# Second attention of a four-layer chain: score units in runs of four and eight, key loads released by scores

## The reference, cut to what matters

```python
q = _rmsnorm((x @ Wq).reshape(B, T, H, D), q_rms_w)     # B 4, T 1024, H 16, D 64
k = _rmsnorm((x @ Wk).reshape(B, T, H, D), k_rms_w)
v = (x @ Wv).reshape(B, T, H, D)
gate = softplus(einsum('bthd,hd->bht', k_raw, u_n) / sqrt(D))
bias = where(idx_i >= idx_j, -(idx_i - idx_j) * omega_h * gate_j, -inf)
scores = einsum('bihd,bjhd->bhij', q, k) / sqrt(D) + bias
y = einsum('bhij,bjhd->bihd', softmax(scores), v).reshape(B, T, H * D)
return y @ Wproj
```

## Time and profile before

| quantity | us |
|---|---|
| median of 3 runs | 2235.26 (2231.14 to 2236.41) |
| profiled execution, its own time | 2221.2 |
| its span, first to last instruction | 2219.4 |
| one group of the second attention, steady | 25.27 |
| TensorE busy over the span | 2040.5 |
| VectorE, ScalarE, GpSimd busy | 1351.3, 1148.5, 841.2 |

### The profile page before, as it was taken

The page is one execution under the profiler, slowest core; times in us unless marked ns, Lnnn a source line. Parts: engine busy times, 40 slices in busy tenths (PEclk is TensorE's granted clock), DMA queues, the critical chain, the costliest instruction groups (busy, mean ns, idle before and its releaser), DMA issues.

```text
span 2219.4 us, 34339 instructions
## 1 busy us (share of the span) xinstructions
PE 2040.5 (92%) x11728; PEld 1162.8 (52%) x11728; DVE 1351.3 (61%) x3316; ACT 1148.5 (52%) x1859; POOL 841.2 (38%) x544
## 2 busy tenths in 40 slices
PE   5799999998587998896999999999999999999998
PEld 2333333333486554553566665656656555656644
DVE  4788888884732777874666676666666664333311
ACT  2366666667343686782455555555555553223222
POOL 5000000001501455442677777777777772000000
PEclk8799999999688999996999999999999999999999
DMA  5233333112275689896666777667776687533300
GB/s 180 100 125 121 127 131 130 60 51 74 97 197 142 207 263 332 265 294 162 153 155 163 177 177 177 156 161 180 173 175 163 157 226 210 116 86 86 91 5 10
DMA packets 260300, 335.88 MB, mean 151 GB/s; under 512 B 22732, under 2 KB 181756, under 8 KB 259720
## 3 DMA queue, kind: packets, MB, share of 16 engines
q1 hardware_dynamic: 244824, 305.82, 51.5%
q0 software_dynamic: 7664, 24.39, 3.0%
q10 hardware_dynamic: 7640, 3.48, 0.6%
HBM read 193.69 MB, written 122.62 MB: 143 GB/s over the span
## 4 chain that ended last, share of the span: by engine, by line
PE 41%; issue 6%; DVE 4%; SPq 2%; DMA 1%; ACT 0%; DVEq 0%
PE ps L1287 10%; PE ps L956 6%; PE ps L940 6%; PE ps L909 6%; PE ps L941 5%; PE ps L1238 2%; DVE a1mx L1012 2%; PE ps L1298 1%; PE ps L1275 1%; PE ps L1276 1%; PE ps L943 1%; DVE a1mx L1008 1%; SPq L1162 1%; DMA a1FQ<-s_q 1%; DVE a1mx L1005 0%
## 5 line engine op out<-in xcount | busy, mean ns | idle before, releaser
L1123 POOL TENSOR_TENSOR a1sum<-a1sum,a1prob 128x1024 f32<-128x1024 f32 (+3 forms) x256 | 462.9, 1808 | 82.6 <-ACT a1prob L1066 50.3
L1066 ACT ACTIVATE a1prob<-ps 128x512 f32<-128x512 f32 (+2 forms) x640 | 327.9, 553 | 243.8 <-PE ps L943 209.8
L479 DVE TENSOR_REDUCE a0grid<-ps 128x8 f32<-128x1024 f32 x288 | 351.1, 1223 | 102.1 <-PE ps L351 64.7
L1005 DVE CUSTOM_DVE_ANT_0 ps<-ps,c_mask_ij 128x128 f32<-128x128 f32 x496 | 264.3, 551 | 195.1 <-issue 190.8
L580 ACT ACTIVATE a0prob<-ps 128x1024 f32<-128x1024 f32 x288 | 286.0, 1024 | 168.4 <-PE ps L377 110.9
L940 PE MATMUL ps<-a1QA,a1KA 69*128 69x512 f32 (+3 forms) x768 | 284.6, 378 | 4.4 <-DMA a1QA<-a1neg 4.4
L956 PE MATMUL ps<-a1prob,a1V 128*64 128x512 f32 (+3 forms) x1536 | 273.1, 498 | 4.5 <-ACT a1prob L1066 4.5
L941 PE MATMUL ps<-a1QB,a1KB 128*128 128x512 f32 (+3 forms) x768 | 263.3, 350 | 0.0
L909 PE MATMUL ps<-a1KA,a1QA 68*128 68x128 f32 x744 | 224.7, 381 | 4.8 <-DMA a1KA<-s_g 3.9
L956 PEld LDWEIGHTS ps<-a1prob,a1V 128*64 128x64 f32 x1536 | 102.8, 138 | 172.1 <-issue 138.2
L1008 DVE TENSOR_REDUCE a1mx<-ps 128x1 f32<-128x320 f32 x248 | 145.9, 588 | 70.5 <-PE ps L909 67.6
(11 more groups left out here) (269 smaller groups left out, 3105.1 us busy)
## 6 DMA issues: line engine op xcount, KB each, us to landing
a1FQ<-s_q SPq DMA_DIRECT2D x128, 256.0 KB, 7.9
a1KB<-s_k SPq DMA_DIRECT2D x128, 256.0 KB, 8.6
s_xs<-c_zero POOLq DMA_DIRECT2D x19, 1024.0 KB, 9.4
s_q<-mqkT SPq DMA_DIRECT2D x32, 512.0 KB, 3.6
s_v<-mv SPq DMA_DIRECT2D x32, 512.0 KB, 5.8
s_k<-a1KH SPq DMA_DIRECT2D x32, 512.0 KB, 5.0
s_k<-a1KL SPq DMA_DIRECT2D x32, 512.0 KB, 5.9
a1KA<-s_k SPq DMA_DIRECT2D x64, 256.0 KB
```

Source lines behind the costliest of these rows:

```text
L479: dve.tensor_reduce(grid[g % 2][:, :, a:b + 1:b - a], banks(("max", k)), axis=AX.X, op=ALU.max).then_inc(s1_free, 1)
L1005: dve.tensor_tensor_reduce(bank[:, 0:w], bank[:, 0:w], const["mask_ij"][:, BANK - w:BANK], 1.0, LOWEST, ALU.add, ALU.max, mx[:, x % 2, h, ...
L1066: act.activation(weights_of(g, u)[:, group[0]:group[-1] + 1, off:BANK], both(e, u, group), ACT.Exp).then_inc(weighed, 1)
L1123: pool.tensor_tensor(t[:, :, off:BANK], t[:, :, off:BANK], weights_of(g, u)[:, :, off:BANK], ALU.add).then_inc(summed, 1)
```

## The change

Units 4 to 11 become one run: scores of eight units with their jobs, then "den", then eight products with V. The turn moves from unit 8 behind the jobs of unit 11 (in group 0, in front of them). ScalarE splits the queries after units 0 and 1 instead of 0 and 3, issues the row's DMA after unit 11 instead of 9, and copies the denominators after unit 11 instead of 7. The buffers of keys, slopes and `QB` are released by the last scores of group g-1; only V still waits for its last product. SyncE's queue is reordered: V has a load of its own behind the key loads, the copies of the queries come at steps 1 and 2 instead of 1 and 4, the loads of `KB` at 3, 5, 6, 7 instead of 1, 3, 5, 7, and the denominators are stored one group later.

```diff
-    runs = [range(r, r + TILES) for r in range(0, NU, TILES)]
+    runs = [range(0, TILES), range(TILES, NU)]
...
-    turn_after = lambda g: TURN if g > 0 else TURN + 1
...
     def jobs(g, u):
         if g == 0:
             found = [("max", x, sum(share0[x - 1][:u]) + k) for x in (1, 2) for k in range(share0[x - 1][u])]
-            return [("turn", 1, 0)] + found if u == turn_after(0) else found
+            return [("turn", 1, 0)] + found if u == NU - 1 else found
         x = g + 2 if u >= TURN else g + 1
         first = sum(share[TURN:u]) if u >= TURN else early + sum(share[:u])
         found = [("max", x, first + k) for k in range(share[u])] if x < G else []
-        if u == TURN and g + 1 < G:
+        if u == NU - 1 and g + 1 < G:
             found.append(("turn", g + 1, 0))
         return found
...
         def load_a(x, h):
-            if x >= NB:
-                nc.sync.wait_ge(valued, unit(x - NB, NU - 1) + 1)
+            released(nc.sync, x)
             nc.sync.dma_start(KA[x % NB][0:dim, h, :].bitcast(F32), heads_of(x, scr["k1"][0])[:, h, :]).then_inc(loaded_e[x % NB], 16)

         def load_b(x, k):
             h, r = divmod(k, 2)
-            if x >= NB:
-                nc.sync.wait_ge(valued, unit(x - NB, NU - 1) + 1)
+            released(nc.sync, x)
             nc.sync.dma_start(KB[x % NB][r * dim:(r + 1) * dim, h, :].bitcast(F32), heads_of(x, scr["k1"][r])[:, h, :]).then_inc(loaded_k[x % NB], 16)

+        def released(engine, x):
+            if x >= NB:
+                engine.wait_ge(scored, piece(x - NB + 1, 0))
...
         def load_e(x):
             b, (n, m) = x % NB, divmod(x, PAIRS)
-            if x >= NB:
-                nc.sync.wait_ge(valued, unit(x - NB, NU - 1) + 1)
+            released(nc.sync, x)
             ...
+        def load_v(x):
+            if x >= NB:
+                nc.sync.wait_ge(valued, unit(x - NB, NU - 1) + 1)
             nc.sync.dma_start(V[b][:, :, :], scr["v1"][n * S:n * S + S, m * P:m * P + P].rearrange("(t p) n -> p t n", p=P)).then_inc(loaded_v[b], 16)
...
             for g in range(G + 1):
                 if g > 0:
                     if g + 2 < G:
                         load_e(g + 2)
                         for h in range(2):
                             load_a(g + 2, h)
+                        load_v(g + 2)
...
-                    if g + 2 < G and g > 0 and k % 2 == 1:
-                        load_b(g + 2, k // 2)
-                    if g + 2 < G and k in (1, 4):
-                        copy_high(g + 2, (1, 4).index(k))
+                    if g + 2 < G and k in (1, 2):
+                        copy_high(g + 2, k - 1)
+                    if g + 2 < G and g > 0 and k in (3, 5, 6, 7):
+                        load_b(g + 2, (3, 5, 6, 7).index(k))
...
-                if g > 0:
+                if g > 1:
+                    store_den(g - 2)
+                if g == G:
                     store_den(g - 1)
...
         def split(x, h):            # ScalarE
                 if h == 0:
                     act.wait_ge(loaded_f[x % 2], (x // 2 + 1) * 16 * PARTS)
-                    if x >= NB:
-                        act.wait_ge(valued, unit(x - NB, NU - 1) + 1)
+                    released(act, x)
...
             for g in range(G):
                 for u in range(NU):
                     exponentials(g, u)
-                    if g + 2 < G and u in (0, 3):
-                        split(g + 2, (0, 3).index(u))
+                    if g + 2 < G and u in (0, 1):
+                        split(g + 2, u)
                     if u == TILES - 1:
                         keep(g, 0)
-                    if u == 2 * TILES - 1 and g > 0:
+                    if u == NU - 1 and g + 1 < G:
+                        row(g + 1)
+                    if u == NU - 1 and g > 0:
                         keep_den(g - 1)
-                    if u == turn_after(g) + 1 and g + 1 < G:
-                        row(g + 1)
                 keep(g, 1)
```

More of the change, by code:

```diff
@@ L797, in load_b @@
             h, r = divmod(k, 2)
+            released(nc.sync, x)
+            nc.sync.dma_start(KB[x % NB][r * dim:(r + 1) * dim, h, :].bitcast(F32), heads_of(x, scr["k1"][r])[:, h, :]).then_inc(loaded_k[x % NB], 16)
+        def released(engine, x):
             if x >= NB:
-                nc.sync.wait_ge(valued, unit(x - NB, NU - 1) + 1)
-            nc.sync.dma_start(KB[x % NB][r * dim:(r + 1) * dim, h, :].bitcast(F32), heads_of(x, scr["k1"][r])[:, h, :]).then_inc(loaded_k[x % NB], 16)
+                engine.wait_ge(scored, piece(x - NB + 1, 0))
         def load_e(x):
+            b, (n, m) = x % NB, divmod(x, PAIRS)
+            released(nc.sync, x)
+            slopes = scr["g1"].rearrange("(a h) n -> a h n", a=4)[:, m * 2:m * 2 + 2, n * S:n * S + S]
+            nc.sync.dma_start(KA[b][EXT:EXT + 4, :, :].bitcast(F32), slopes).then_inc(loaded_e[b], 16)
+        def load_v(x):
             b, (n, m) = x % NB, divmod(x, PAIRS)
@@ L807, in load_e @@
                 nc.sync.wait_ge(valued, unit(x - NB, NU - 1) + 1)
-            slopes = scr["g1"].rearrange("(a h) n -> a h n", a=4)[:, m * 2:m * 2 + 2, n * S:n * S + S]
-            nc.sync.dma_start(KA[b][EXT:EXT + 4, :, :].bitcast(F32), slopes).then_inc(loaded_e[b], 16)
             nc.sync.dma_start(V[b][:, :, :], scr["v1"][n * S:n * S + S, m * P:m * P + P].rearrange("(t p) n -> p t n", p=P)).then_inc(loaded_v[b], 16)
@@ L852, in sync_program @@
             load_e(1)
+            load_v(1)
             for k in range(PARTS):
@@ L857, in sync_program @@
             load_e(2)
+            load_v(2)
             for k in range(N_K):
```

## The result

The changed kernel takes 2273.16 us (median of 4 runs, 2264.90 to 2285.05) against 2233.20 for the kernel before (4 runs): a ratio of 1.0184, 95% interval 1.0157 to 1.0211. It is slower, as forecast, but 3 us outside the range that was given (2230 to 2270). The difference of the medians is 40 us, where 21.3 was forecast. The profiled execution after has its own time of 2264.9 and a span of 2263.1 us.

What follows compares the result with a forecast made beforehand. TensorE was taken to bound the kernel. 29 groups at +0.75 us (21.8) less 0.5 gave +21.3, so 2221.2 became 2242.5; the median's 14.1 offset made 2256 us, range 2230 to 2270.

Steps and rivals of the forecast that it cites:

- the sum: Whole kernel: 21.8 us for later groups less 0.5 at the end, +21.3 us, giving 2256 us.
- Start: Group 0: splits delay unit 3 by 1 us, its own 0.9 wait at the turn goes; zero, plus or minus 2.
- The wait: Units 8 to 11 and denominators: TensorE held by VectorE's late maxima; +0.84 us a group worked out, 0.75 taken.
- rival B: Join issued where no GpSimd add runs, taking 0.3 us; VectorE does not decide, 2228 us; chance 0.16.
- signs of being wrong: Join at 0.3 us, VectorE's unit 8 jobs under 1.5 us after TensorE's, or VectorE waits under 0.9 us a group.
- The term for 29 groups: Groups 1 to 29: 0.75 us each for TensorE's waits on VectorE, 21.8 us.
- Splits, row, copies of queries, denominators' copy: Moved splits, row DMA, query copies and ScalarE's copy of denominators: each costs nothing; query copies' slack called thin.
- The rule of the Trainium skill: At the join: waiting for a whole GpSimd add, 2.36 us, would cost 49 us; measured rows give 21.8.
- End: After the last products: the chain to the final loads starts 0.5 us sooner, minus 0.5 us.
- Rival D: Second copy of queries or the row lands 1 us late, adding 29 us: about 2285 us; chance 0.08.
- rival C: Bank waits overlap with unseen gains and cancel, within 0.3%, 6.7 us, of no change; chance 0.14.

## Why the prediction was wrong

**The step that failed is the sum.** It took the clock of 1.00 from the earlier trace rows as given for groups that would wait longer, and has no term for the clock. The long groups cost 20.4 of the 33.6 us in the middle stretch. The rows of steady groups bore no price for it, since before no steady group waited so. But group 0 of the kernel before did, and its trace had the price. TensorE's timeline there, then a window (stretch, us, busy of each engine, PEclk, DMA share, GB/s):

```profile
1056.95 0.27 PE L912 MATMUL ps<-c_ident,a1mx 128*16 128x128 f32 x1 [0.87 <-DVE a1mx L1012]
...
1061.57 4.20 PE L956 MATMUL ps<-a1prob,a1V 128*64 128x512 f32 x16
```

```profile
1059.00:1065.00 6.00, 6.00 (x21) 3.30 (x21) 4.28 (x13) 0.77 (x2) 1.99 (x2) 0.50 0.01 1
```

After a wait of 0.87 us for the join the clock fell to 0.50, at 1058.5 and for 6.8 us, and the sixteen products of units 8 to 11 took 4.20 us instead of the 2.37 of the earlier trace rows. The prediction used the wait of this group (0.9, under "Start") and not the fall behind it. There too a wait does not always bring a fall: the short join in the kernel before has one (0.73 us, fall at 1068.3), the loads alone have none (0.85 us).

That the fall hangs on the wait is shown from both sides: with 0.24 or 0.7 us of work in it the steady groups stay at 25.74 and the falls are gone from the traces; with 0.6 us more of wait 23 of 29 groups have one.

**The wait was in the right place, and its cost was put too high.** The join under GpSimd's add (1.43), the jobs of unit 8 at its heels, the wait at unit 9's first job and at the denominators all came as worked out, and rival B's condition arose in group 0 alone (a join of 0.17). None of the signs of being wrong came: VectorE's jobs of unit 8 start 1.62 us after TensorE's (1406.57 and 1404.95), and in the group from 1113.31 the weight loads of L923 and L935 wait 1.6 us for VectorE, where 1.5 was foretold. The size was 0.47 us a group where 0.84 was worked out and 0.75 taken. With the prediction's times less 2.91 (its join starts at 1408.12, this one at 1405.21) the denominators were to start at 1410.54, and they start at 1410.30: VectorE did not slip before unit 10 (0.11), and they start 0.66 after its second job there, where 0.79 was counted for the job, the bank and the weights. And the products take 5.74 in one piece, not 3.58 + 2.31 = 5.89: the seam between two runs of products was counted though it is gone. 0.24 + 0.15 is the difference from 0.84 to 0.45. The term for 29 groups is 13.6, not 21.8.

**Step by step, the rest.**
- Splits, row, copies of queries, denominators' copy at nothing: right. With the loads alone nothing moves, and from the join of group 1 to that of group 29 TensorE waits for no transfer. The slack of the copies that was called thin is what the change bought: with the copies as before they are 3 to 4 us late.
- The rule of the Trainium skill, "SBUF — State Buffer", "SBUF: two separate sides", on the port of VectorE and GpSimd did not change the sum, but it named the cure, since it speaks of operations with two inputs in SBUF: with one the join does not wait. The runs agree, 0.17 against 1.43 us with the same add under way.
- Start, "zero, plus or minus 2": it was +4.8 to group 1's join, and this is the clock too. TensorE ran at 0.50 until 1069.3, through nearly all of group 0, where before the clock rose at 1041.4. From the first score to the join of group 1 it is 65.4 to 67.4 us in the four traces in which the clock rose at 1069 or later, and 57.5 to 61.7 in the nine in which it rose between 1041 and 1057. The second trace of the kernel after is one of the nine (1050.2 and 61.58 us, against 60.99 before), so in it the term of zero held. What makes the clock rise late is open.
- End, "minus 0.5": it was +2.2, within what this part varies by between the kernels (from the last join to the end it is 405 to 410 us in eleven traces, 406.6 before and 408.7 after).
- Rival D's late transfer and rival C's cancelling gains: neither.

What is not shown is why the clock falls in 7 or 10 groups and not in all, though the wait is the same in each (0.39 to 0.42 us ahead of unit 9's first job).

**The version that wins** is two runs with a short join, with or without the moved denominators: 2217 to 2218 against 2232.6 to 2233.4. So the two runs are worth 0.3 to 0.4 us a group (24.84 or 24.94 against 25.27) when nothing hangs on the join.

## What to carry to other kernels

Ask of a stall covered by other work when the cover moves, and price the clock with it: the waits behind the join cost here 0.9 us a group by themselves (25.74 against 24.84 with the denominators in them) and 0.7 a group, on average, through the clock. Look for that price in the start and the end of a stage too, where its steady part doesn't show it. Where an engine must be waited for, put work of TensorE's there that has to be done anyway; here the denominators, 1.0 us, gave back some 50 us by standing one place earlier. A VectorE instruction that ends each time with one of GpSimd's should lose its second SBUF input before its place is tuned.

## What the runs showed of the hardware

- A maximum of two SBUF tiles of 8 elements a partition took 1.43, 0.73 or 0.17 us, by how much of GpSimd's add of 2.39 us was still to run; a reduction of 16 elements from one tile took 0.17 with an add under way.
- In the kernel after, the granted clock fell to 1.2 GHz 1.4 to 1.7 us after a wait of some 0.4 us plus the weight load behind it, for about 6.8 us, though TensorE was busy for 25.07 of 25.72 us in a steady group. The Trainium skill, "TensorE: Matmul & The Clock Gate", "A second HAM failure mode: psum-queue depth-cycling", describes another kernel, whose matmuls cycle through PSUM banks and in which short idle times of TensorE between groups of them come often enough to make the clock swing; the trace agrees in kind, with seven falls in 28 groups.
- The other way round the clock was slow to come: in group 0 of the kernel after it stayed at 0.50 from 1042 to 1066 with TensorE busy in the whole of it, while in the second trace of the same kernel it was at 1.00 from 1050.2. This window is of the first:

```profile
1048.00:1054.00 6.00, 6.00 (x16) 4.23 (x16) 4.40 (x20) 1.96 (x4) 4.53 (x2) 0.50 0.63 174
```
